# Scores by token tile and five single PSUM banks in the first stage of a fused transformer kernel

## What is computed

```python
x = x + attn_a(layernorm(x))       # 8 heads of 64; keys and values through a latent of rank 64
x = x + ffn(layernorm(x))          # two layers: local attention (window 128), then a gated MLP
x = x + attn_b(layernorm(x))       # 16 heads of 16, causal, rational scores
x = x + ffn(layernorm(x))          # two layers again

# attn_a
scores = jnp.einsum('bqhd,bkhd->bhqk', q, k) * scale
attn = jax.nn.softmax(scores, axis=-1)
out = jnp.einsum('bhqk,bkhd->bqhd', attn, v)
```

## Time and profile before

| | |
|---|---|
| median of 3 runs | 4717.62 us (4715.44 to 4721.88) |
| the profiled execution, its own time | 4717.21 us |
| its span (first to last instruction) | 4715.3 us |
| PE busy | 4207.5 us, 89% of the span |
| DVE busy | 3324.7 us, 71% |
| ACT busy | 2555.6 us, 54% |
| POOL busy | 1603.4 us, 34% |
| mean granted TensorE clock | 0.948 of full speed |

### The profile page before, as it was taken

The page is one execution under the profiler, slowest core; times in us unless marked ns, Lnnn a source line. Parts: engine busy times, 40 slices in busy tenths (PEclk is TensorE's granted clock), DMA queues, the critical chain, the costliest instruction groups (busy, mean ns, idle before and its releaser), DMA issues.

```text
span 4715.3 us, 65711 instructions
## 1 busy us (share of the span) xinstructions
PE 4207.5 (89%) x23120; PEld 2616.4 (55%) x23120; DVE 3324.7 (71%) x7849; ACT 2555.6 (54%) x5482; POOL 1603.4 (34%) x1816
## 2 busy tenths in 40 slices
PE   7888888999999999988888878888999999999997
PEld 4545455655655655655555455554565665665654
DVE  5555566676676676648899999988677666667662
ACT  4444444444444444437888888876444444444441
POOL 2122235454454554430000010012554454454441
PEclk9999999999999999997888898888999999999998
DMA  2000000000001000000000000100000000000000
GB/s 72 10 5 15 18 5 12 3 5 3 21 10 28 7 10 12 18 17 19 21 21 21 17 26 21 32 19 18 19 3 5 3 22 10 28 16 19 12 19 20
DMA packets 63094, 78.31 MB, mean 17 GB/s; under 512 B 15344, under 2 KB 47520, under 8 KB 62768
## 3 DMA queue, kind: packets, MB, share of 16 engines
q1 hardware_dynamic: 62768, 74.12, 5.5%
HBM read 36.37 MB, written 12.58 MB: 10 GB/s over the span
## 4 chain that ended last, share of the span: by engine, by line
PE 67%; DVE 19%; ACT 6%; issue 5%; POOL 2%; DMA 0%; SPq 0%; POOLq 0%; DVEq 0%; ACTq 0%
PE wide L782 48%; PE o_ps L782 8%; PE turn_ps L785 6%; PE wide L785 4%; DVE x L1213 3%; DVE w_up L1326 2%; DVE prob L1338 2%; DVE x L1332 2%; PE turn_ps L782 1%; DVE w_up L1311 1%; POOL prob L1542 1%; DVE hid L1332 1%; DVE resid L1398 1%; DVE x L1430 1%; DVE k_t L1273 1%
## 5 line engine op out<-in xcount | busy, mean ns | idle before, releaser
L782 PE MATMUL wide<-x,w_up 128*128 128x512 f32 (+5 forms) x2560 | 864.4, 549 | 27.8 <-DVE x L1430 20.6
L782 PE MATMUL wide<-w_in,x_t 128*128 128x512 f32 (+2 forms) x1920 | 818.0, 570 | 57.1 <-ACT turned L1076 43.8
L1542 POOL TENSOR_SCALAR prob<-prob,st 128x256 f32<-128x256 f32 (+1 forms) x1024 | 449.3, 459 | 989.2 <-DVE st L1362 988.7
L1145 ACT ACTIVATE prob<-prob,st 128x256 f32<-128x256 f32 (+1 forms) x1024 | 479.4, 472 | 315.6 <-DVE st L1349 315.6
L782 PEld LDWEIGHTS wide<-w_in,x_t 128*128 128x128 f32 x1920 | 344.1, 193 | 411.1 <-issue 403.5
L782 PEld LDWEIGHTS wide<-x,w_up 128*128 128x128 f32 (+2 forms) x2560 | 370.9, 195 | 297.9 <-issue 253.1
L782 PE MATMUL o_ps<-pt,v 128*32 128x128 f32 (+2 forms) x5120 | 508.8, 345 | 26.6 <-DVE pt L1375 10.2
L785 PE MATMUL turn_ps<-ident,prob 128*128 128x128 f32 x2480 | 407.4, 283 | 93.5 <-issue 40.3
L1515 POOL TENSOR_TENSOR sines<-raw,rot 128x512 f32<-128x512 f32 x256 | 352.4, 1397 | 334.8 <-ACT raw L1073 334.8
L785 PEld LDWEIGHTS turn_ps<-ident,prob 128*128 128x128 f32 x2480 | 285.2, 142 | 319.5 <-issue 247.5
L1523 POOL TENSOR_TENSOR rn<-ss,minus_half 128x16 f32<-128x16 f32 x128 | 410.0, 3203 | 151.8 <-DVE ss L1259 145.0
(11 more groups left out here) (139 smaller groups left out, 7362.1 us busy)
## 6 DMA issues: line engine op xcount, KB each, us to landing
kept<-resid SPq DMA_DIRECT2D x16, 512.0 KB, 2.6
x<-kept SPq DMA_DIRECT2D x16, 512.0 KB, 3.3
w_up<-hid SPq DMA_DIRECT2D x64, 128.0 KB, 2.2
x<-hid SPq DMA_DIRECT2D x64, 128.0 KB, 2.4
shifted<-resid SPq DMA_DIRECT2D x32, 224.0 KB
w_in<-in_f_wqkv SPq DMA_DIRECT2D x4, 1536.0 KB, 6.9
w_up<-in_f_w SPq DMA_DIRECT2D x4, 1492.0 KB, 7.5
resid<-in_x SPq DMA_DIRECT2D x8, 512.0 KB, 8.6
```

The source lines that it names most:

```text
L782: return eng.matmul(out, lhsT, rhs, start=start, stop=stop, skip_group_check=True)
L1145: last = eng.activation(pr[:, local_span(t)], pr[:, local_span(t)], ACT.Exp, bias=sm[:, t:t + 1], scale=-1.0, accum_out=sm[:, 4 + t:5 + t])
L1542: last = eng.tensor_scalar(pr[:, local_span(t)], pr[:, local_span(t)], sm[:, 8 + t:9 + t], 1.0, ALU.mult, ALU.mult)
```

## The change

First, in stage a the banks are given out differently. The planner keeps a list of the holders of seven banks; wide0 stays a pair (A_PAIRS = 1) for "xt", "lat", "aq", "proj", while the four banks of wide1 and wide2 and turn_ps are five single banks, any of which "score", "turn_a" and "turn_b" may take. "score", "low" and "exp" of stage a now go by token tile: a part is one head and one tile, 512 columns, in one bank. `tile_part(k, t)` numbers them. The matmuls, exponentials, transposes and copies stay the same in number and size; the reduction of 1024 columns becomes two of 512. The planner's assumed durations are set to match (score 1.0, low 0.62, exp 0.75).

Second, `readers_of` drops "exp" from the readers of a score of stage f, so the plan counts its pair as held until "low" alone. No instruction or wait of stage f is altered by this; only the order and the choice of buffers can be. The last lines of `parts_of` in the diff drop conditions that follow from others.

```diff
+A_PAIRS = 1
+def tile_part(k, t):
+    return k // 2 * 4 + 2 * t + k % 2
...
-        scaled = [("wt", *old["st"]), ("inv", *old["st"]), ("exp", *old["st"])] if old["st"] else []
+        scaled = [("exp" if stage_of(old["st"][0]) == "b" else "wt", *old["st"])] if old["st"] else []
...
-            else:
-                put("score", k, at, final("aq_c", 1), final("ak_c"))
-            put("low", k, at, final("score", k | 1), *scaled, *(turned if st == "f" else []))
+                put("low", k, at, final("score", k | 1), *scaled, *turned)
+            elif k % 2:
+                for t in range(2):
+                    for step in (k - 1, k):
+                        i = tile_part(step, t)
+                        freed = [(kind, *BEFORE[u, step][of]) for kind, of in
+                                 (("wt", "st"), ("turn_a", "prob"), ("turn_b", "prob")) if BEFORE[u, step][of]]
+                        put("score", i, at, final("aq_c", 1), final("ak_c"))
+                        put("low", i, at, final("score", i | 1), *freed[:1])
+                        put("exp", i, at + 1 / steps, final("low", i), *freed[1:])
...
+BANKS = 7
+def rooms(part):
+    kind, u, i = part
+    st = stage_of(u)
+    pairs, single = [(f"wide{k}", (2 * k, 2 * k + 1)) for k in range(3)], (f"bank{BANKS - 1}", (BANKS - 1,))
+    if st == "a" and kind in ("score", "turn_a", "turn_b"):
+        return [single] + [(f"bank{k}", (k,)) for k in range(A_PAIRS * 2, BANKS - 1)]
+    if kind in NARROW and not (kind == "turn_a" and st == "b"):
+        return [single]
+    return pairs[:A_PAIRS] if st == "a" else pairs
+
+def readers_of(part):
+    kind, u, i = part
+    last = [(r, u, 0 if kind in ("proj", "down") else i) for r in READERS[kind]]
+    if kind == "turn_a" and stage_of(u) == "b":
+        last.append(("pt_b", u, i))
+    if kind == "score" and stage_of(u) == "f":
+        last.remove(("exp", u, i))
+    return last
...
-    rings = {"wide": [None] * 3, "narrow": [None]}
+    holders = [None] * BANKS
...
-        for k, holder in enumerate(rings[ring]):
+        for name, banks in rooms(part):
             at = 0.0
...
+            for holder in {holders[k] for k in banks} - {None}:
+                for r in readers_of(holder):
+                    if r in parts:
+                        at = max(at, end[r] + HOP) if at is not None and r in end else None
+            if at is not None and (best is None or at < best[0]):
+                best = (at, name)
...
-                if HELD.get(part):
-                    psum_read(pe, HELD[part])
+                for held in HELD.get(part, ()):
+                    psum_read(pe, held)
...
-                    pair, half = i // 4, i // 2 % 2
-                    for k in range(2):
-                        t = 2 * half + k
-                        for j in (0, 1):
-                            r = slice(64 * j, 64 * j + 64)
-                            last = mm(wide[PLACE["score", u, i - 1 + j]][:, k * 512:(k + 1) * 512],
-                                      q_t[s][r, pair, t * P:(t + 1) * P], k_t[s][r, 0, :], True, True)
-                            if k == 1:
-                                last.then_inc(S["score"], 1)
+                    pair, t = i // 8, i // 2 % 4
+                    for j in (0, 1):
+                        r = slice(64 * j, 64 * j + 64)
+                        mm(buffers[PLACE["score", u, i - 1 + j]][:, :], q_t[s][r, pair, t * P:(t + 1) * P], k_t[s][r, 0, :],
+                           True, True).then_inc(S["score"], 1)
...
-                    for k in range(2):
-                        cut = slice(k * 512, k * 512 + 512)
-                        last = eng.activation(pr[:, cut], ps[:, cut], ACT.Exp, bias=sm[:, k:k + 1],
-                                              accum_out=sm[:, 2 + k:3 + k])
-                    last.then_inc(S["exp"], 1)
+                    eng.activation(pr[:, t * 512:t * 512 + 512], buffers[PLACE["score", u, i]][:, :], ACT.Exp,
+                                   bias=sm[:, t:t + 1], accum_out=sm[:, 2 + t:3 + t]).then_inc(S["exp"], 1)
...
-                    eng.tensor_reduce(sm[:, 0:2], wide[PLACE["score", u, i]][:, :].rearrange("p (t n) -> p t n", t=2), AX,
-                                      ALU.max, negate=True).then_inc(S["low"], 1)
+                    eng.tensor_reduce(st[SLOTS[u, step]["st"]][:, t:t + 1], buffers[PLACE["score", u, i]][:, :], AX, ALU.max,
+                                      negate=True).then_inc(S["low"], 1)
```

## The result

The changed kernel takes 4520.2 us (median of 4 runs, 4514.7 to 4522.2) against 4717.4 us for the kernel before: the ratio is 0.958, with a 95% interval of 0.956 to 0.960. The direction was right, and the waits that were named went in both parts; both sizes were too small, that of the f stages by far.

A forecast was written before the change was run, and what follows sets the result against it. PE was taken to bound the kernel, its first-stage idle time being waits before transposes. -75 us there and -25 us in the f stages gave 4717 - 100 = 4617 us; own range 4592 to 4640, with rivals 4580 to 4668.

The forecast's parts named there:

- Bound and mechanism: First stage: PE sets the pace; its idle time is waits before transposes into the single turn_ps, at most 83.0 us removable.
- Rival 2: First stage: another engine sets the round, 6.75 instead of 6.25 us, keeping 32 us of waits; 4645 us, chance 0.12.
- rival 3: First stage: the plan keeps turned weights on one bank, so the 83 us stay; about 4692 us, chance 0.03.
- 5: F stages: slower than before, PE waits for the normalised input because its filler is taken sooner; 4742 us, chance 0.03.
- Room: First stage: five single banks should suffice, a round needing 20 of 31 bank-us by token tile, 30 with the old holds.
- What is left idle: First stage: 10 us of PE idle time taken to remain, between bounds of 0 and 27 us.
- Maxima of 512 columns: First stage, DVE: halved reductions cost 0 to 0.16 us more a step, at most 20 us, beside PE's work.
- Stage a's sum: First stage: 83 us of waits removed, 10 us idle left, 2 us gained by clock: -83 + 10 - 2 = -75 us.
- The clock: First stage: a rise from 0.98 to 1.00 gains at most 11 us; 2 us taken.
- The f stages: F stages: removing waits for line 1076 gains between 46 us and a loss of 20; 25 us taken.
- rival 4: First stage: cycling through five banks lowers TensorE's clock to 0.87, losing 60 of the 75 us; 4677 us, chance 0.03.
- The largest case I priced: Whole kernel: no first-stage idle, clock at 1.00 and all 46 us in f, -140 us, 4577 us; chance 0.04.

The follow-up runs named there:

- turns_one: Changed kernel, but first-stage transposes keep to turn_ps alone and scores by token tile use the four banks of wide1 and wide2; 4591.6 us, ratio 0.973.
- turns_three: Kernel before, but first-stage transposes may take any of three single banks; scores stay whole steps in pairs, two pairs for all other kinds; 4768.5 us, ratio 1.009.
- pairs_two: Changed kernel with two pairs and three single banks in the first stage in place of one pair and five singles; 4654.6 us, ratio 0.985.
- f_rooms: Kernel before, instruction order unchanged; only the choice among the three pairs made again, local scores counted free after their maxima; 4659.1 us, ratio 0.986.
- f_only: Kernel before with only the second part: the plan counts a local score of the f stages as held until the maxima; 4640.9 us, ratio 0.982.
- f_half: Kernel before with the second part alone, for the first two f stages only; 4681.4 us, ratio 0.990.
- a_only: Changed kernel without the planner's new rule for local scores, so only the first part; 4606.8 us, ratio 0.976.
- mix_cost: Changed kernel with the planner's assumed duration of a first-stage mix set to 1.9 us in place of 2.4; 4520.7 us, ratio 0.956.
- singles_four: Changed kernel with four single banks in the first stage in place of five; 4543.4 us, ratio 0.962.
- f_turn_rooms: Changed kernel, but transposes of the f stages may also take a free pair, not turn_ps alone; 4829.3 us, ratio 1.023.

## Why the prediction was right or wrong

*Bound and mechanism: right in the main.* PE set the pace, its idle time stood before transposes, and the waits went. But the prediction gave the whole of it to the room, and finer scores a part only in whether the room suffices; turns_one shows that they remove about half of the waits by themselves, and turns_three that room without them, taken from the pairs, makes the stage slower. DVE took no hold of the round: it is busy 333.6 of 482.2 us, 69%, where I had 71. Rival 2 is out, and so are 3 and 5. (Rival 2's own figure was off: 32 us kept, in place of the 10 that I left, give 4639 us, or 4649 on top of them, not 4645.)

*Room: right for five banks.* In the round shown a score bank is held 2.6 to 3.6 us where I estimated 3 to 4. My figure for the kernel before was too high: I gave all four score banks 6.0 us, but the first two are held 4.6, so the demand was 2 x 4.6 + 2 x 6.0 + 6 = 27 bank-us, not 30. How much a shortage costs I did not see: in rival 3 I put 83 us on it, and with three banks (pairs_two) stage a is longer by 143 us than with five.

*What is left idle: right.* 10 us forecast; 10.7 found in the first stretch, 2.5 more in the eighth unit.

*Maxima of 512 columns: right.* The reduction takes 0.679 us against 1.218 for 1024, so a step costs 2 x 0.679 - 1.218 = 0.14 us more, beside PE's work. The estimate by the Trainium skill (VectorE: DVE Perf Modes, "The TRN2 errata") was 0.125.

```profile
L1387 DVE TENSOR_REDUCE st<-wide 128x1 f32<-128x512 f32 x213 | 134.6, 679 | 8.6 <-PE wide L821 7.6 <-PE turn_ps L821 0.4
```

*Stage a's sum: too small, -75 for -107.* The idle term was nearly right: -83 + 10 = -73, where idle time fell by 70.7 us in the first stretch and 9.8 in the eighth unit, 80.5 in all. The step that failed is the pricing of a removed wait at its idle time alone. "PE gets no instruction" was right, but from it the prediction took PE's busy time to stay, but for 2 us of clock. Busy time fell by 26 us (28.0 in the first stretch, with 1.8 more in the eighth unit). The transposes' share, 30 us, is a term that the sum did not have, put at nothing without a reason. The clock was mis-sized: 2 taken, up to 11.6 found in the first stretch, my upper bound, and in the eighth unit, where it rose from 0.94 to 1.00, up to 0.06 x 92 = 5.5 us.

*The f stages: wrong, -25 for some -90.* The step that failed is the ceiling: "All of it can go" took the 46.4 us for line 1076 as the most there was, and discounted it to 25 for the risk of another order. As a ceiling of idle time from this wait it held: with the order unchanged (f_rooms) idle time in the f stages falls by 45.4 us. But the time falls by 61, because busy time falls too (by 17 us in the two pairs of f stages), which the prediction again put at nothing. And the new order did not lose: I expected it to be short of work before the normalised input ("the work pulled forward would be missing there"). It was not: that wait fell from 63.2 to 45.7 us over the run, and the "qk" wait went to 3.0:

```profile
  DVE ss L1288: 82.5, 34
  PEld wide L824: 3.5, 3
  PE wide L821: 3.0, 3
```

(who waited for the square, line 1111 of the changed kernel, as the last of the earlier trace rows). Idle time of PE fell by 32.5 and 32.6 us in the two pairs of f stages, 65 in all. The remaining 30 us lie in busy time (8.5 and 21.3 us; in f_only 15.4 and 23.0, with 52 us of idle time gone). The clock of these stretches is 0.99 in both kernels and 1.00 in f_only, so it may be part of this; how much is clock, how much the grouping of instructions and how much the cutting of the stretches stays open.

*Clock: rival 4 is out.* Stage a now cycles PE through five banks, and the granted clock is 1.00. The Trainium skill (TensorE: Matmul & The Clock Gate, "A second HAM failure mode: psum-queue depth-cycling") tells of a kernel in which cycling through banks came with small idle times and a clock that rose and fell; here the small idle times, and the lower clock of 0.96 to 0.98, belong to the kernel with one bank for the transposes.

*Range and chances.* 4580 to 4668 missed. The largest case I priced, 4577, added every upper bound I had and still lay 57 us off: but for the clock, the bounds were of the waits alone. The 0.94 for faster was right.

## What to carry to other kernels

A wait for a buffer on the bounding engine can cost more than its idle microseconds. Here 71 us of idle time brought 99 us, because the transposes, in longer stretches, also took less busy time and the clock was higher; in f_rooms 45 us brought 61. So the idle sum is no ceiling of the gain. It is no sure floor either: in turns_one 37 us of idle time brought 30, because busy time rose by 7. Before giving a buffer class more room, compute holding time times count against banks times round, and shorten the holds first: more banks for the transposes went with -107 us where scores were freed by the tile, and with +53 where they were not; scores by the tile with only three shared banks came to +36 (pairs_two). Here such a count of bank-us told where four banks would do and three would not, but not what a shortage costs. Check a planner's release rule against the wait the code really makes: a stale reader in a table cost 1.8% of the time here (f_only), without a single instruction being wrong.

## What the runs showed of the hardware

The granted clock of stage a differs between executions with the same waits. In f_only, f_rooms, f_half and the kernel before, the idle time of PE up to the seventh unit is 81.4 to 81.5 us; the clock is 0.96, 0.97, 0.97 and 0.98, and the stretch lasts 591.2, 589.3, 588.2 and 580.9 us. In the executions whose idle time there is 10 to 13 us (changed kernel, a_only, mix_cost, singles_four, f_turn_rooms) it is 1.00 each time. Between and beyond lie turns_one (44.1 us idle, 0.99), pairs_two (86.5, 0.96) and turns_three (119.6, 0.93). So in these runs the clock is lower where PE idles more, but at one and the same idle time it still varies. The stretch of f_only, to set beside that of the kernel before:

```profile
40.00:631.20 591.20, 509.79 (x2829) 292.57 (x2828) 337.77 (x580) 271.86 (x655) 132.96 (x135) 0.96 0.03 10
```

Up to 10 us of difference between two gapped kernels of this kind are thus no effect of an edit. The profiled execution of the kernel before has the highest clock of the four, so the 107 us of stage a would have been larger against one of the other three, by up to 10 us.
